# One pre-norm decoder layer: cross attention and feed-forward merged into one software-pipelined loop

## The reference

```python
# cross attention (ctx 128 wide, one head of 256)
q = query @ Wq + bq;  k = key @ Wk + bk;  v = value @ Wv + bv
out = softmax(q k^T) v
# feed-forward: 8 adapters (rank 16), top 2 of a softmax gate
scores = softmax(hidden @ gate_w.T + gate_b);  top_v, top_i = top_k(scores, 2);  val_sum = top_v.sum(-1)
for e in range(8):
    gate  = (top_i == e).sum(-1) * val_sum
    inter = hidden @ wi.T + bi + (hidden @ lora_A[e].T) @ lora_B[e].T
    out  += gate * (relu(inter) @ wo.T + bo)
x = x + block(layernorm(x))
```

## Time and profile before

| | us |
|---|---|
| median of 3 runs (lowest, highest) | 930.27 (928.88, 931.19) |
| the profiled execution | 931.96 |
| its span, first to last instruction | 930.2 |
| granted TensorE clock, mean over the span | 0.835 of full |

### The profile page before, as it was taken

How to read it: one execution, slowest core, us unless ns; L and a number is a source line. 1 busy time by engine, 2 the same in 40 slices (tenths; PEclk the granted TensorE clock), 3 DMA queues, 4 the chain that set the end, 5 groups by cost and what they waited for, 6 DMA issues and landing times. The chain is left out here.

```text
span 930.2 us, 22413 instructions
## 1 busy us (share of the span) xinstructions
PE 694.4 (75%) x8314; PEld 630.3 (68%) x8314; DVE 585.0 (63%) x1467; ACT 335.6 (36%) x797; POOL 296.3 (32%) x313
## 2 busy tenths in 40 slices
PE   4785885756664467665656675499999999999997
PEld 3664764655554356565545564399999999999997
DVE  5654642222222677775888887568877888887773
ACT  4463641112112444441433333133444333434432
POOL 0222310000003988872334342023333323233322
PEclk9997985555565577777888878589999999999999
DMA  8387796455641233341222222000011000001000
GB/s 239 85 170 196 192 203 81 71 93 98 105 122 48 79 103 101 101 124 46 74 69 73 68 73 80 23 13 23 25 31 38 23 23 23 23 23 45 13 13 24
DMA packets 95271, 71.04 MB, mean 76 GB/s; under 512 B 31192, under 2 KB 91872, under 8 KB 95200
## 3 DMA queue, kind: packets, MB, share of 16 engines
q1 hardware_dynamic: 94240, 66.89, 28.4%
q10 hardware_dynamic: 960, 3.15, 1.9%
HBM read 40.66 MB, written 29.36 MB: 75 GB/s over the span
## 5 line engine op out<-in xcount | busy, mean ns | idle before, releaser
L1164 ACT ACTIVATE f_h<-banks,bic 128x256 f32<-128x256 f32 x256 | 102.1, 474 | 83.0 <-PE banks L630 65.9
L1677 POOL TENSOR_TENSOR f_hs<-f_h 128x512 f32<-128x512 f32 x64 | 85.6, 1349 | 135.4 <-ACT f_h L1164 131.8
L1316 DVE TENSOR_TENSOR h_sm<-banks,blockmask 128x1024 f32<-128x1024 f32 x32 | 37.7, 1219 | 114.6 <-PE banks L741 114.6
L1598 POOL TENSOR_TENSOR m_rh<-m_ms,mhalf 128x32 f32<-128x32 f32 x16 | 88.3, 5517 | 1.3
L1548 DVE CAST f_hT_hi<-f_hs 128x512 fp32r<-128x512 f32 x64 | 44.1, 689 | 62.3 <-POOL f_hs L1677 62.3
L630 PE MATMUL banks<-f_adT_hi,lbT_lo 128*128 128x256 f32 x256 | 72.8, 284 | 12.4 <-ACT f_h L1164 12.4
L630 PE MATMUL banks<-woT_hi,f_hT_lo 128*128 128x256 f32 x256 | 74.5, 291 | 1.0 <-DVE f_hT_lo L1550 1.0
L759 PE MATMUL banks<-h_sm,h_v 64*16 64x64 f32 x2048 | 36.7, 297 | 50.1 <-issue 50.1
L630 PE MATMUL banks<-f_xT_hi,wiT_lo 128*128 128x256 f32 x256 | 73.0, 285 | 0.3 <-DVE f_adT_lo L1540 0.3
L630 PE MATMUL banks<-woT_lo,f_hT_hi 128*128 128x256 f32 x256 | 71.5, 279 | 0.0
L630 PE MATMUL banks<-f_xT_lo,wiT_hi 128*128 128x256 f32 x256 | 71.5, 279 | 0.0
(11 more groups left out here) (253 smaller groups left out, 2160.4 us busy)
## 6 DMA issues: line engine op xcount, KB each, us to landing
qk_scratch<-p_qk SPq DMA_DIRECT2D x32, 256.0 KB, 2.4
h_qk<-qk_scratch SPq DMA_DIRECT2D x20, 256.0 KB, 8.9
xin<-in_x_dram SPq DMA_DIRECT2D x8, 512.0 KB, 5.1
v_scratch<-p_v SPq DMA_DIRECT2D x16, 256.0 KB, 4.1
h_v<-v_scratch SPq DMA_DIRECT2D x16, 256.0 KB, 8.1
attn_scratch<-h_wn SPq DMA_DIRECT2D x16, 256.0 KB, 5.3
m_w<-attn_scratch SPq DMA_DIRECT2D x16, 256.0 KB, 2.8
m_x<-in_x_dram SPq DMA_DIRECT2D x16, 256.0 KB, 2.9
```

The costliest lines, as they stand in the source:

```text
L1164: ins = act.activation(out_slot[:, j % 2, c * T:(c + 1) * T], bank[4 + j][:, c * T:(c + 1) * T], ACT.Relu, bias=bic[:, f:f + 1])
L1316: dve.tensor_tensor(h_sm[:, r, 2 * s:2 * s + 2], pairs[s][:, :, :], blockmask[:, :].rearrange("p (o n) -> p o n", o=1).broadcast_to([P, 2, ...
L1598: pool.tensor_tensor(out_ap, tmp, mhalf[:, 0:width], ALU.pow).then_inc(done, 1)
L1677: pool.tensor_tensor(f_hs[:, j % 2], f_h1[:, j % 2], f_h2[:, j % 2], ALU.add).then_inc(f_hsd, 1)
```

## The change

Cross attention and feed-forward become one loop over the 16 units (20 steps). Unit u has its moments and normalisation for cross attention in step u, the whole of its cross attention in step u + 1, its normalisation, adapters, gate and masks in step u + 2, its hidden layer in step u + 3 and `fed` in step u + 4. x2 stays in SBUF (no x2_scratch). With it:

- Both normalisations move from DVE to ACT (Identity with scale rstd and bias -mean*rstd); POOL makes the bias by two more small instructions.
- The constant of the scores: product on POOL, sum by a DVE reduce (before: two accumulating DVE instructions).
- The second relu on ACT and the sum on POOL become one DVE pass from the bank: `total`, max(bank, -bias) + relu1, two instructions per j. The missing bias goes into a row bi @ wo^T, made once.
- The high part of the hidden layer moves from DVE to ACT (`high`), the low part from DVE to POOL (`remainder`). The high part of the masked adapters moves from DVE to ACT.
- Most double buffers and second banks go; banks are shared between the two blocks.
- Between heads and mix PE computes the row bi @ wo^T: 16 fp32 matmuls (not split) of 256 columns in `bank[7]`, and ACT copies it out ahead of its first mix instruction; DVE prepares the operand (8 instructions) behind the heads.

The diff, cut to its core:

```diff
+            pe.wait_ge(s_bwide, 1)
+            for f in range(FT):
+                for part in range(2):
+                    ins = pe.matmul(bank[7][:, 0:D], spread[:, f, :], woT[part][:, f, :].bitcast(F32),
+                                    start=f == 0 and part == 0, stop=f == FT - 1 and part == 1)
+            ins.then_inc(s_brow, 1)
...
+            act.wait_ge(s_brow, 1)
+            act.activation(brow[:, :], bank[7][:, 0:D], ACT.Copy).then_inc(s_browd, 1)
...
+            def normalised(u, nmrd, mean_rstd, rstd, src, dst, done):
+                act.wait_ge(nmrd, nth(u, 1, 1))
+                for i in range(TT):
+                    ins = act.activation(dst[:, i], src[:, i], ACT.Identity, bias=mean_rstd[:, i:i + 1], scale=rstd[:, i:i + 1])
+                ins.then_inc(done, 1)
...
+            def high(j):
+                def emit(u):
+                    act.wait_ge(f_hsd, nth(u, 4, j + 1))
...
+                    act.activation(flat(f_hT[0][:, 2 * j:2 * j + 2, :]), f_hs[:, j % 2], ACT.Copy).then_inc(f_hhi, 1)
...
+            def total(j):
+                def emit(u):
+                    dve.wait_ge(f_more, nth(u, 4, j + 1))
+                    dve.wait_ge(f_h1d, nth(u, 4, j + 1))
...
+                    for c in range(2):
+                        f = 2 * j + c
+                        ins = dve.scalar_tensor_tensor(out=f_hs[:, j % 2, c * T:(c + 1) * T], in0=bank[4 + j % 3][:, c * T:(c + 1) * T],
+                                                       scalar=nbic[:, f:f + 1], in1=f_h1[:, j % 2, c * T:(c + 1) * T],
+                                                       op0=ALU.max, op1=ALU.add)
+                    ins.then_inc(f_hsd, 1)
...
             def c_moments(u):
-                moments(u, 0, c_x, c_st, c_mv)
+                dve.wait_ge(c_xin[u.slot], landed(u))
+                if u.has(1):
+                    dve.wait_ge(c_nmrd, nth(u, 1, 0))
+                moments(u, c_stats, c_x[:, u.slot], c_st, c_mv, c_var)
...
+            def scales(u, step_sem, var, mv, tmp, rs, nm, rstd_done, mean_done):
+                rstd(u, step_sem, (var, nth(u, 1, 1)), mv[:, :, 1], 1.0, LN_EPS, tmp, rs, TT, rstd_done)
+                pool.wait_ge(rstd_done, nth(u, 1, 1))
+                apart(pool)
+                for i in range(TT):
+                    ins = pool.tensor_scalar(nm[:, i:i + 1], mv[:, i, 0:1], rs[:, i:i + 1], -1.0, ALU.mult, ALU.mult)
+                ins.then_inc(mean_done, 1)
...
+            def remainder(j):
+                def emit(u):
+                    pool.wait_ge(f_hhi, nth(u, 4, j + 1))
...
+                    pool.tensor_tensor(lo, f_hs[:, j % 2], hi.bitcast(F32), ALU.subtract).then_inc(f_hlo, 1)
```

More of the change, by code:

```diff
@@ L299, in decoder @@
         with ExitStack() as a:
[L300 removed]
+            borow = sb("borow", [P, D], F32, a)
+            nbic = sb("nbic", [P, FT], F32, a)
             c_x = sb("c_x", [P, 2, TT, D], F32, a)
             c_c = sb("c_c", [P, 2, TT, C], F32, a)
[L303 to L308, removed]
[L309 to L314 removed]
+            c_st = sb("c_st", [P, TT, 6], F32, a)
+            c_mv = sb("c_mv", [P, TT, 2], F32, a)
+            c_ve = sb("c_ve", [P, TT], F32, a)
+            c_rs = sb("c_rs", [P, TT], F32, a)
+            c_nm = sb("c_nm", [P, TT], F32, a)
+            c_xn = sb("c_xn", [P, TT, D], F32, a)
+            c_rr = sb("c_rr", [P, TT, D], F32, a)
+            c_r = sb("c_r", [P, TT], F32, a)
+            c_xT = pair("c_xT", [P, KD, T], a)
+            c_ch = pair("c_ch", [P, TT, C], a)
+            c_cT = pair("c_cT", [P, T], a)
+            c_uT = pair("c_uT", [P, T], a)
             c_mx = sb("c_mx", [P, TT], F32, a)
@@ L812, in _, with turn_cx @@
             pe.wait_ge(m_yd, UNITS)
+            def turn_cx(u):
+                pe.wait_ge(c_norm, nth(u, 1, 1))
+                if u.has(1):
+                    pe.wait_ge(c_olo, nth(u, 1, 0))
+                turn(bank[0], c_xn).then_inc(c_turned, 1)
             def turn_context(u):
@@ new lines, in second @@
+            def second(j):
+                def emit(u):
+                    pe.wait_ge(f_h1d, nth(u, 4, j + 1))
+                    for c in range(2):
+                        ins = product(pe, bank[4 + j % 3][:, c * T:(c + 1) * T],
+                                      lambda p: lbT[p][:, (2 * j + c) * P:(2 * j + c + 1) * P],
+                                      lambda p: f_adT[u.slot][p][:, 1, :], False, True, True)
+                    ins.then_inc(f_more, 1)
+                return emit
@@ L1154, in f_exps @@
                 if u.has(1):
-                    act.wait_ge(f_xbd, nth(u, 1, 0))
+                    act.wait_ge(f_vsd, nth(u, 1, 0))
                 act.activation(flat(f_ex[:, :, :]), flat(f_sh[:, :, :]), ACT.Exp).then_inc(f_exd, 1)
-            def relus(u, j, ready, out_slot, done, back):
-                act.wait_ge(ready, nth(u, 4, j + 1))
-                if j >= 2 or u.has(1):
-                    act.wait_ge(f_hsd, nth(u, 4, j - 1))
-                for c in range(2):
-                    f = 2 * j + c
-                    ins = act.activation(out_slot[:, j % 2, c * T:(c + 1) * T], bank[4 + j][:, c * T:(c + 1) * T],
-                                         ACT.Relu, bias=bic[:, f:f + 1])
-                ins.then_inc(done, 1)
@@ new lines, in relu @@
+            def relu(j):
+                def emit(u):
+                    act.wait_ge(f_base, nth(u, 4, j + 1))
+                    if j >= 2 or u.has(1):
+                        act.wait_ge(f_hsd, nth(u, 4, j - 1))
+                    for c in range(2):
+                        f = 2 * j + c
+                        ins = act.activation(f_h1[:, j % 2, c * T:(c + 1) * T], bank[4 + j % 3][:, c * T:(c + 1) * T],
+                                             ACT.Relu, bias=bic[:, f:f + 1])
+                    ins.then_inc(f_h1d, 1)
+                return emit
```

489 lines of the change are left out of this document (207 added, 282 removed).

## The result

The changed kernel takes 1011.88 us (median of 4 runs, 1009.59 to 1016.74), the kernel before 929.58 (4 runs, 926.44 to 931.19). The ratio is 1.0897 with a 95% interval of 1.0846 to 1.0947: about 9% slower. 971 was forecast, with a range up to 998. The sign was right, and so was the ring through the queues that the forecast describes; the size was not, and the clock, which had been kept out of the sum, takes part in it.

What follows compares the result with a forecast made beforehand. The order of the queues was taken to bound the merged loop at 31.9 us a step: 513.3 us to the fourth turn_cx, 382.8 for 12 full steps and 74.7 to the end give 970.8, 971 as median; range 940 to 998.

Steps and rivals of the forecast that it cites:

- the ring: Merged loop: chain through the engine queues from turn_cx to the next turn_cx, 30.7 us a step, 31.9 with contention.
- third to fourth: Third to fourth turn_cx, a step without fed: 31.9 less 2.8, so 29.1 us.
- the 12 full steps: Merged-loop steps with all the work: 12 at 31.9 us, 382.8 us in all.
- last turn_cx to the end: Draining of the merged loop: steps of 27.4, 21.4, 16.5 and 9.4 us, sum 74.7.
- (a): PE's work from turn_cx to the end of second(1), with a 0.6 us loss at turn_f: 16.45 us.
- (b): DVE's work in a row from total(1) to total(2), including c_olow's wait for ACT: 9.7 us.
- the hold: POOL's remainder(1) holds up DVE's comparisons in f_rank: 1.2 us a step, bounds 0 and 1.3.
- (c): Tail over POOL and ACT to the next turn_cx: high, remainder, 1/sqrt, c_normalise and hand-overs, 4.6 us.
- a rival of its own: Rival 2: PE's clock falls in the step's sparse part, 3 to 5 us at half speed; 997 us, chance 0.21.
- rival 1: No hold of DVE in f_rank: 14 steps x 1.2 us less, 954 us; chance 0.21.
- The bias row: 16 fp32 matmuls and ACT's copy between heads and mix: 5.5 us on the path; matmuls 3.4 to 8.
- Rival 3: PE sets the step, about 23.5 us, 862 us total; decides from 28.8 us a step on; chance 0.13.

Runs made afterwards that it cites:

- experiment 1: Changed kernel with c_moments, the 1/sqrt and normalisation of cross attention moved to earlier places in the three queues: 968.13 us, ratio 1.0382.
- Experiments 5 and 6: 5: 24, 18 and 16 useless matmuls in the changed kernel's three PE waits, 997.32 us; 6: 18 and 9 added to experiment 1, 953.71 us.
- experiment 3: Changed kernel with ACT copying the bias row out behind its mix loop instead of ahead of it: 1005.82 us, ratio 1.0791.
- experiment 4: Changed kernel with remainder(1) on POOL waiting in addition until f_rank has made its masks: 1007.83 us, ratio 1.0816.
- experiments 7 to 10: 7: experiment 1, step end reordered, 933.86 us; 8: 7 with experiments 3, 4, 916.43; 9: 8, f_normalise earlier, 914.76; 10: 9, f_gate later, 909.30.

## Why the prediction was right in kind and wrong in size

The profiled span is 1015.0 where 970.8 was forecast, 44.2 us more (that execution was the slowest of its four; by the medians the miss is 41). By the terms of the sum, from the starts of turn_cx in the trace:

| term | forecast | measured | off by |
|---|---|---|---|
| first turn_cx | 442.2 | 446.2 | +4.0 |
| first to third | 42.0 | 41.8 | -0.2 |
| third to fourth | 29.1 | 33.6 | +4.5 |
| the 12 full steps | 382.8 | 409.3 | +26.5 |
| last turn_cx to the end | 74.7 | 84.1 | +9.4 |

**The ring.** The order of the queues was read rightly: the same three parts, closed at the same place, and experiment 1 shows that taking away the closing link brings back 48 of the 82 us lost. (The waits it removed are part of that, and so is the slow stretch behind turn_cx.) In a step at full clock, from 829.58 to 862.67 in the rows above:
(a) turn_cx to total(1): 17.35 against 16.45. The wait ahead of turn_f is 0.76 instead of 0.6. The rest is nearly all PE's own work, 16.4 us for the 138 instructions instead of 15.7: those of the hidden layer follow each other at 0.1175 us in the mean rather than 0.1135, and the first ones behind transposes are further apart. The hand-over to DVE was priced rightly: total(1) starts 0.31 us after the start of the last matmul of second(1), which leaves 0.19 where 0.15 was taken.
(b) total(1) to the end of total(2): 10.55 against 10.9 (9.7 and the hold). The hold is 0.95 instead of 1.2.
(c) to the next turn_cx: 5.2 against 4.6. c_ve to the end of c_nm takes 1.75 where I had 1.45, and the pair c_xn takes 1.09 where I had 0.87.
Together 33.1 against 31.95. None of these is large, and 12 of them make 14 us. That is the first step that failed: in (a) and (c) I priced PE's work and the small instructions at their best case. c_xn is the clearest: I took about the duration of a pair of f_h, which reads PSUM and has one pointer operand; c_xn reads SBUF and has two, and one instruction takes 592 ns. The Trainium skill ("ScalarE: Activation LUTs", "What ACT_TABLE_LOAD costs") would have given it: an activation with a pointer as bias at some 280 ns and 0.833 ns an element, and 93 ns more for each further pointer; from these figures an estimate for 256 elements and two pointers is 586 ns. The trace agrees, with 583 to 600.

**The clock.** This is the second step that failed, about as large as the first, and it is an error of form. I made it a rival of its own, at 0.21, and put it at nothing in the forecast, though rival and forecast do not exclude each other: the gaps that the ring forces on PE are what the clock falls behind. Experiments 5 and 6 fill the gaps and the clock goes to 1.00; that takes away about 1 us a step in the mean, 12 us in the 12 full steps, and with the steps around them 15 to 17 us of the miss. The third to the fourth turn_cx alone takes 29.9 us in experiment 5 instead of 33.6. The size, 2 us a step, was right for the steps that are slow behind turn_cx; toward the end only each second one is. "PE is busy 71% of the new step, and most of it in one stretch", which I gave as the argument against, did not hold: behind a step with gaps of 2.2, 2.1 and 3.4 us the clock fell all the same. The Trainium skill's rule ("TensorE: Matmul & The Clock Gate", "What's actually happening"), the throttled state as the default that activity releases, agrees with this.
The experiments also corrected me in the other direction: after experiment 1 I put all of the missing 2.5 us a step down to the clock. Experiment 5 left 1.2 of them, which (a) to (c) account for. And a slow stretch costs less than its length where PE has to wait for DVE soon after anyway: behind turn_cx it costs 2.1 us a step; behind turn_masks, where crossed still waits for c_oT_lo, 1.1 (experiments 1 and 6); and behind crossed, where turn_cx waits for the ring anyway, nothing (the step from 862.67 to 897.84 above).

**The hold (rival 1 denies it).** Right that it is there, wrong that 1.2 us a step hang on it. The rows show 0.95, and experiment 4 that only 0.2 to 0.3 come back at full clock, since POOL's instruction then holds f_top. Rival 1 would have forecast 17 us from it; 7.5 were measured with the slow steps that it spared. The size of the hold is what POOL has left to do. The pair of f_eq at 849.00 starts 0.29 us into this POOL instruction and ends 0.22 us behind it, which is the time of the second comparison alone:

```profile
848.71 1.38 POOL L1659 TENSOR_TENSOR f_hT_lo<-f_hs,f_hT_hi 128x512 fp32r<-128x512 f32 x1 [2.50 <-ACT f_hT_hi L1156]
```

The Trainium skill ("SBUF — State Buffer", "Who interferes with whom") was the better guide here than the rows of the other direction: the comparisons are held up, and to the end of POOL's instruction. (One POOL instruction that reads SBUF does not hold DVE, against that rule: see the last section.) The same hold lies on f_sh in every full step, 0.87 to 1.13 us instead of 0.17 before, and in the step above it costs nothing, as forecast: DVE waits 0.69 us for PE behind it.

**The bias row.** 5.5 forecast, 8.7 by the first square of mix (8.3 by the means over all kernels), 10 us by the ratios of experiment 3. The row was misread: x4 there is two products. What was measured lies beyond the upper bound of 8 too. The clock was 1.00, so with two records for each product the price is 6.9 us and ACT's copy. The number of products that the code issues there (two, L669) against the count in the row would have shown it.

**The end.** +9.4: the step that begins with the last turn_cx took 33.4 us to the next first(0), not 27.4, and the one after it 25.1, not 21.4. I had let them run through at full clock with the waits of (b) only; the trace has masks waiting 2.4 and 2.8 us there, and first products at half speed behind them. Two other traces separate this. In experiment 5, at a clock of 1.00, the first of these steps takes 29.5 us, and so it does in experiment 3, whose loop is the changed kernel's own and has no slow stretch behind this turn_cx. So 3.9 us are the clock, and whether they are lost differs between executions; 2.1 are the ring. The step after it takes 25.7 in both, over 4 us more than forecast, with the clock down behind its wait for the masks in all three traces (there is no filler in that step); how much of the 4 us is that stretch stays open. The end is 80.8 us in both.

**Rival 3** had the right condition, as far as the experiments can show it: it decides from 28.8 us a step on, and experiments 7 to 10, at 28.3 to 27.5, lie at and below the time before (8 to 10 also without the wait for the row). Its 23.5 us was never reached: PE itself has 24.3 us of work in the fastest version's step, and the remaining 3 are its waits for other engines.

## What to carry to other kernels

When loops are merged to fill an engine, follow one step around through every queue and look for the instructions of the next unit that stand last on an engine: the moments, the 1/sqrt and the normalisation of cross attention at the ends of three lists cost 48 us here, more than half of the loss, and another order of the same work made the merged loop faster than the two loops before. Count the gaps that the ring leaves on PE and charge them for the clock in the forecast itself: filling one of three gaps only moved the half-speed stretch, closing them all took it away. A half-speed stretch costs only what the next wait does not swallow. And price the small things at what a row of the same form shows (source in SBUF or PSUM, pointer operands, number of records for each product), because a ring adds up a dozen of them, each step.

## What the hardware showed that was not expected

Useless matmuls made the kernel faster: 58 more a step, 15 us less (experiment 5).

A POOL instruction of 1.3 us delays even the smallest DVE instruction with two operands in SBUF, until POOL has finished: f_top, 16 elements, took 0.89 us instead of 0.16 (experiment 4). But POOL's 1/sqrt of 5.5 us, a TENSOR_TENSOR with both inputs in SBUF, delays none: an m_a starts beside it in 14 of the 16 units, and every m_a takes 0.69 us. In the mix loop of the changed kernel:

```profile
324.56 5.52 POOL L1570 TENSOR_TENSOR m_rh<-m_ms,mhalf 128x32 f32<-128x32 f32 x1
324.83 0.69 DVE L1336 TENSOR_TENSOR m_a<-m_t,m_at 128x512 f32<-128x512 f32 x1
...
325.44 0.69 DVE L1315 TENSOR_TENSOR m_n<-m_w,m_rh 128x512 f32<-128x512 f32 x1
```

So it is not the length of the POOL instruction that counts here. That its 32 elements are soon read, and that only the reading holds DVE, is an inference that no run here tries.
